# Sixteen-head cross attention: one exponential per score bank, the next scores behind the first of a unit's two, and another order of an item's jobs

## The chip, the cores and the metric

The kernel runs on one core of a Trainium2 chip. The metric is the device time of one execution in microseconds (us). TensorE (PE) multiplies matrices, with its weight loads listed apart as PEld; VectorE is DVE, ScalarE is ACT, GpSimd is POOL, and SyncE (SP) issues transfers. The engines run their own queues in order and meet at semaphores.

## What is computed

The whole program is two layers of a perceiver: x holds 32 items of 64 tokens by 128 features, and the context `ctx_1024` holds 32 items of 1601 tokens by 128. The change touches one of its six parts, the cross attention of the second layer with 16 heads of 8 features:

```python
H, dk = (N_HEADS, D_K)            # 16, 8
Q = (x_q @ W_Q + b_Q).reshape(B, L, H, dk).transpose(0, 2, 1, 3)
K = (x_k @ W_K + b_K).reshape(B, S, H, dk).transpose(0, 2, 1, 3)
V = (x_v @ W_V + b_V).reshape(B, S, H, dk).transpose(0, 2, 1, 3)
scores = jnp.einsum('bhld,bhsd->bhls', Q, K) / jnp.sqrt(jnp.float32(dk))
attn = jax.nn.softmax(scores, axis=-1)
ctx = jnp.einsum('bhls,bhsd->bhld', attn, V)
out = ctx.transpose(0, 2, 1, 3).reshape(B, L, H * dk) @ W_O + b_O
```

Here `x_q` is the normalized x (L = 64) and `x_k`, `x_v` are the context (S = 1601), for B = 32 items. The other parts are an eight-head cross attention, two self attentions, a mixture of experts and a tree network.

## The kernel before

`cross_attention` serves the eight-head stage (`XA0`) and the sixteen-head stage (`XA1`). It goes through 32 items (`b`). The 1601 context tokens are 13 tiles of 128 (the last has 65). With 16 heads the scores of one tile against 64 tokens are 16 x 64 = 1024 columns, two banks of PSUM, and one tile is one **unit**: an item has `NE` = 13 units. The work of an item is cut into jobs, and the string `ORDERS[heads]` lists them:

- S x: `pe_scores` (L585 with 16 heads, L589 with 8), eight matmuls for unit x, four into each of its two banks; then ACT's `act_exp` (L636) reads both banks with one instruction of 1024 columns and writes the buffer `Pb`.
- P x: `pe_product` (L605), probabilities times values of unit x, summed over the item in one bank. P-1 is the last unit of the item before.
- M j: `pe_maxima` (L552), raw scores of 402 keys (or 395) for the next item, into two banks; DVE reduces them to maxima in `dve_maxima`, with one instruction where the two banks are neighbours (L709) and two where they are not (L706, L707). There are 16. After M15 `dve_shift` makes the shift of the exponent, and job R (`pe_shift_rows`, L568, copied by ACT L687 and DVE L732) puts it in as rows of the queries.
- V j: `pe_values` (L538), values of four tiles for the next item, evicted by ACT (L656). V0, V1 and V2 have four tiles each, V3 has one.
- K j: `pe_keys` (L523), keys for the item after the next, evicted by ACT (L646) and then by DVE (L695). The letter H marks DVE's part.

Every engine walks the same string and takes its own part of each job, so the string fixes the order on PE, ACT and DVE, and for POOL and SP the places at which they prepare and load. Nothing is reordered at run time: an instruction that waits holds up all behind it on its engine. ACT's part of S x is `act_exp`; at P-1 it copies out the item's sums (`act_output`, L668), once an item. SP issues the key transfers of an item (L772, L773) at H3 and a context load (L761) at V3.

The eight PSUM banks are split with 16 heads into 3 for scores, 1 for the sums and 4 for work (M, V, K, R), which go round in a ring; an M job takes two of them, so two M jobs can be in flight. An item takes 41 work banks, so its jobs sit one bank further in the next. The scores' ring has three banks: unit u uses banks 2u and 2u + 1 modulo 3. Two units need four banks, and `pe_scores` waits until the whole exponential of the unit before has ended:

```python
emptied_exp = unit(b, x) - (1 if att.score_banks == 3 else 2)
if emptied_exp >= 0:
    eng.wait_ge(exps, units + emptied_exp + 1)
```

`act_exp` also waits for the product of four units before, since `Pb` has four buffers. With 8 heads there are four score banks, and the wait reaches back two units.

Of the kernel before, what the change touches and what calls it, by code (L numbers as in the profile page):

```python
# [37 lines left out]
ROWS = 98  # L38
# [8 lines left out]


ORDERS = {
# [4 lines left out]

# [1 line left out]
class Attention:  # L56


    def __init__(self, name, heads, cross, masked=False, values_k=D):
# [25 lines left out]
        self.NE = len(self.exps)  # L85
        self.units = heads // 2
        self.halved = heads == 16
        q4 = 402
        self.kchunks = [(c * q4, min(q4, NK - c * q4)) for c in range(4)] if cross else []
        self.vjobs = [list(range(i, min(i + 4, len(self.tiles)))) for i in range(0, len(self.tiles), 4)]  # L90
# [103 lines left out]
def bass_perceiver_kernel(nc, xT, ctxT, wpack, bpack, experts, picks, trees, outT):  # L194
    ROUTED = nc.dram_tensor("routed", (E, N), F32, kind="Internal").ap()
    ctx = ExitStack()
    with ctx:
# [245 lines left out]
        def cross_attention(role, eng, att, part, bname, inputs_ready=None, banks_ready=None):  # L443
# [58 lines left out]
            def unit(b, x):  # L502
                return b * NE + x

            def score_banks(b, x):

                first, last = sorted((2 * unit(b, x) + i) % att.score_banks for i in range(2))
                return ps[:, first:last + 1:last - first, :]

            def buffer(b, x):  # L510
                return unit(b, x) % 4
# [60 lines left out]
            def pe_scores(b, x):  # L572
                if x == 0:
                    for by in att.freed[(b, "R", 0)]:
                        eng.wait_ge(*emptied((b, "R", 0), by))
                emptied_exp = unit(b, x) - (1 if att.score_banks == 3 else 2)
                if emptied_exp >= 0:
                    eng.wait_ge(exps, units + emptied_exp + 1)
                out = score_banks(b, x)
                for ti, tile in enumerate(att.exps[x]):  # L580
                    k0, n = att.tiles[tile]
                    for g in range(4):
                        if att.halved:
                            for h in range(2):
                                mm = nc.tensor.matmul(out[0:n, h, g * 128:(g + 1) * 128], KST[half[h], b % 3, g, k0:k0 + n],  # L585
                                                      QW[half[h], b % 3, g * 128:(g + 1) * 128], start=True, stop=True,
                                                      tile_position=(64 * h, 0))
                        else:
                            mm = nc.tensor.matmul(out[0:n, ti, g * 128:(g + 1) * 128], KST[0:ROWS, b % 3, g, k0:k0 + n],  # L589
                                                  QW[0:ROWS, b % 3, g * 128:(g + 1) * 128], start=True, stop=True)  # L590
                mm.then_inc(scores, 1)

            def pe_product(b, x):
                if x == 0:
# [2 lines left out]
                        eng.wait_ge(oev, items + b)  # L597
                    else:
                        eng.wait_ge(vones, 2 * past + 2)
                eng.wait_ge(exps, units + unit(b, x) + 1)  # L600
                for ti, tile in enumerate(att.exps[x]):
                    _, n = att.tiles[tile]
                    for r, quad, h0, nh, v0, oc in att.groups:
# [26 lines left out]
            def act_exp(b, x):  # L630
                n = att.tiles[att.exps[x][0]][1]
                banks = len(att.exps[x]) * att.W // 512
                if unit(b, x) >= 4:
                    eng.wait_ge(pv, units + unit(b, x) - 3)
                eng.wait_ge(scores, units + unit(b, x) + 1)
                nc.scalar.activation(Pb[0:n, buffer(b, x), 0:banks * 512].rearrange("p (a c) -> p a c", a=banks),  # L636
                                     score_banks(b, x)[0:n, 0:banks, :], ACT.Exp, scale=att.scale).then_inc(exps, 1)

            def act_keys(b, j):
                job = (b, "K", j)  # L640
# [1566 lines left out]
```

## Time and profile before

| | us |
|---|---|
| Median of 3 runs | 1993.44 |
| Lowest and highest | 1987.66, 1996.09 |
| Profiled execution, its own time | 1998.57 |
| Its span, first to last instruction | 1996.8 |
| Mean granted clock of TensorE, share of full | 0.944 |
| PE, DVE, ACT, POOL busy | 1784.8, 1389.0, 1228.5, 506.3 |

The profile is of one execution. A busy time is the time in which an engine had at least one instruction running. In timelines the first two numbers of a row are the start and the duration, "xN" is how many instructions were merged into it, and the bracket gives the engine's idle time before it with what released it. The stage of the change runs from about 1003 to 1719 us of the span.

### The profile page before, as it was taken

Reading aid. Unit: us, or ns where it says so; the run is one execution under the profiler, and the core shown is the slowest. Engines: PE = TensorE matmul, PEld = TensorE weight load, DVE = VectorE, ACT = ScalarE, POOL = GpSimd, SP = SyncE. Lnnn points to the kernel's source line nnn. Section 1 sums busy time; section 2 is a strip of 40 time slices with the busy share of each in tenths; the row PEclk is TensorE's granted clock in tenths of the full one; section 3 lists DMA queues with packets and bytes.
Section 4 is the critical chain, followed back from the end, with each engine's and each line's share of the span. In section 5 each row is a group of like instructions: output and inputs, shape, how many; then the busy total and the mean of one; then the engine's idle time right before and its main releaser. Section 6 shows DMA issues by size and latency. Waiting matters only on the chain. (4 is left out here: it accounts for less than half of the span.)

```text
span 1996.8 us, 67986 instructions
## 1 busy us (share of the span) xinstructions
PE 1784.8 (89%) x29656; PEld 1112.0 (56%) x29656; DVE 1389.0 (70%) x2411; ACT 1228.5 (62%) x1789; POOL 506.3 (25%) x399
## 2 busy tenths in 40 slices
PE   7899999999999576998599999999999998857898
PEld 5577777777755454443355555555555555525543
DVE  2577777777636654665688888888888887337565
ACT  3377777777733552332278777877787777338243
POOL 4322323222131511112112222222222220024265
PEclk8799999999999687999799999999999999778999
DMA  4355555555300301654645554555555551030011
GB/s 151 95 139 149 143 150 136 144 147 140 75 2 6 60 3 43 169 146 145 114 73 96 97 94 87 101 94 97 89 101 91 96 92 28 1 65 4 28 37 43
DMA packets 66549, 178.33 MB, mean 89 GB/s; under 512 B 20276, under 2 KB 24500, under 8 KB 65844
## 3 DMA queue, kind: packets, MB, share of 16 engines
q1 hardware_dynamic: 64436, 170.85, 38.9%
q8 instruction: 234, 3.83, 0.8%
q10 hardware_dynamic: 1824, 3.20, 0.8%
q14 instruction: 55, 0.45, 0.1%
HBM read 84.39 MB, written 1.31 MB: 43 GB/s over the span
## 5 line engine op out<-in xcount | busy, mean ns | idle before, releaser
L636 ACT ACTIVATE Pb<-ps 128x1024 f32<-128x1024 f32 (+2 forms) x640 | 630.5, 1001 | 187.2 <-PE ps L585 139.5
L709 DVE TENSOR_REDUCE MX<-ps 128x2 f32<-128x804 f32 (+1 forms) x386 | 369.0, 985 | 51.3 <-PE ps L552 46.6
L605 PE MATMUL ps<-Pb,V 128*17 128x64 f32 (+1 forms) x13312 | 365.2, 249 | 0.2 <-ACT Pb L636 0.2
L605 PEld LDWEIGHTS ps<-Pb,V 128*17 128x17 f32 (+1 forms) x13312 | 251.8, 98 | 83.5 <-issue 69.4
L711 DVE TENSOR_REDUCE MX<-ps 128x1 f32<-128x402 f32 (+1 forms) x512 | 265.6, 568 | 30.2 <-PE ps L556 24.2
L753 POOL TENSOR_TENSOR ABO<-CT 128x1601 bf16<-128x1601 f32 x44 | 125.9, 2863 | 565.6 <-DMA CT<-ctxT 565.6
L552 PE MATMUL ps<-KST,QW 50*128 50x402 bf16 (+1 forms) x1024 | 176.1, 342 | 22.4 <-ACT V L656 11.1
L585 PE MATMUL ps<-QW,KST 50*128 50x128 bf16 (+1 forms) x3328 | 167.1, 220 | 30.9 <-ACT Pb L636 23.9
L585 PEld LDWEIGHTS ps<-QW,KST 50*128 50x128 bf16 (+1 forms) x3328 | 96.4, 96 | 125.6 <-ACT Pb L636 93.1
L656 ACT ACTIVATE V<-ps 128x512 f32<-128x512 f32 (+1 forms) x256 | 130.9, 514 | 40.2 <-PE ps L538 30.2
L556 PE MATMUL ps<-KST,QW 96*128 96x402 bf16 (+1 forms) x512 | 148.4, 339 | 5.5 <-DVE C L695 0.7
L538 PE MATMUL ps<-WS,ABO 128*128 128x128 bf16 (+1 forms) x832 | 132.3, 220 | 0.0
L589 PE MATMUL ps<-QW,KST 98*128 98x128 bf16 (+1 forms) x1664 | 124.5, 219 | 2.1 <-ACT Pb L636 1.6
L695 DVE SCALAR_TENSOR_TENSOR HL<-ps,W,HL 128x402 bf16<-128x402 f32 (+1 forms) x128 | 77.1, 632 | 60.6 <-ACT HL L646 58.8
L538 PE MATMUL ps<-WS,CT 128*128 128x128 bf16 (+1 forms) x1144 | 117.5, 222 | 0.1
L589 PEld LDWEIGHTS ps<-QW,KST 98*128 98x128 bf16 (+1 forms) x1664 | 108.5, 99 | 16.3 <-ACT Pb L636 2.3
L695 DVE SCALAR_TENSOR_TENSOR C<-ps,W,C 128x402 bf16<-128x402 f32 (+1 forms) x128 | 77.1, 632 | 51.4 <-ACT C L646 49.1
L552 PEld LDWEIGHTS ps<-KST,QW 50*128 50x128 bf16 x1024 | 51.2, 93 | 97.0 <-issue 40.5
L538 PEld LDWEIGHTS ps<-WS,CT 128*128 128x128 bf16 (+1 forms) x1144 | 89.2, 100 | 22.9 <-issue 8.9
L1549 ACT ACTIVATE Pb<-ps 128x512 f32<-128x512 f32 x68 | 40.5, 597 | 98.3 <-PE ps L1509 92.8
L1509 PE MATMUL ps<-ABO 128*128 128x512 bf16 x384 | 95.4, 385 | 3.7 <-DVE Pb L1558 3.7
L523 PE MATMUL ps<-CT,WS 128*128 128x402 bf16 (+1 forms) x336 | 90.4, 351 | 6.0 <-ACT V L656 5.5
(246 smaller groups left out, 2986.3 us busy)
## 6 DMA issues: line engine op xcount, KB each, us to landing
CT<-ctxT SPq DMA_DIRECT2D x44, 800.5 KB, 4.8
KST<-HL SPq DMA_DIRECT2D x320, 100.1 KB, 2.9
KST<-C SPq DMA_DIRECT2D x320, 100.1 KB, 3.0
Pb<-routed SPq DMA_DIRECT2D x64, 256.0 KB, 4.0
ABO<-ctxT SPq DMA_DIRECT2D x10, 800.5 KB, 5.3
T<-ctxT SPq DMA_DIRECT2D x10, 800.5 KB, 4.5
KST<-HL SPq DMA_DIRECT2D x128, 50.0 KB, 2.7
KST<-C SPq DMA_DIRECT2D x128, 50.0 KB, 2.7
```

Of the source, the lines that this page charges most:

```text
L538: mm = nc.tensor.matmul(work(job)[0:n, i * D:(i + 1) * D], still[:, k0:k0 + n], WS[:, 1, wp, :], start=(k == 0), stop=(k == 2))
L552: mm = nc.tensor.matmul(work(job)[:, h, 0:n], QW[half[h], b % 3, g * 128:(g + 1) * 128], KST[half[h], b % 3, g, c0:c0 + n], start=True, st ...
L556: mm = nc.tensor.matmul(work(job)[:, 0:n], QW[0:RAW, b % 3, g * 128:(g + 1) * 128], KST[0:RAW, b % 3, g, c0:c0 + n], start=True, stop=True)
L585: mm = nc.tensor.matmul(out[0:n, h, g * 128:(g + 1) * 128], KST[half[h], b % 3, g, k0:k0 + n], QW[half[h], b % 3, g * 128:(g + 1) * 128], ...
L589: mm = nc.tensor.matmul(out[0:n, ti, g * 128:(g + 1) * 128], KST[0:ROWS, b % 3, g, k0:k0 + n], QW[0:ROWS, b % 3, g * 128:(g + 1) * 128], s ...
L605: mm = nc.tensor.matmul(ps[32 * quad:32 * quad + m, SUM, oc:oc + nh * S], V[0:n, b % 2, tile, v0:v0 + m], Pb[0:n, buffer(b, x), ti * att.W ...
L636: nc.scalar.activation(Pb[0:n, buffer(b, x), 0:banks * 512].rearrange("p (a c) -> p a c", a=banks), score_banks(b, x)[0:n, 0:banks, :], AC ...
L656: nc.scalar.activation(V[0:n, b % 2, ts[0]:ts[0] + len(ts), 0:att.NV].rearrange("p t (h e) -> p t h e", h=att.H)[:, :, :, 0:att.d], work(j ...
L695: nc.vector.scalar_tensor_tensor(keys(b)[:, 1, c0:c0 + n], work(job)[:, 0:n], bias(f"bk{t[-1]}"), keys(b)[:, 0, c0:c0 + n], ALU.add, ALU.s ...
L709: nc.vector.reduce_max(MX[:, b % 2, 2 * j:2 * j + 2], work(job)[:, :, 0:n], AX.X).then_inc(freed["dve"], 1)
L711: nc.vector.reduce_max(MX[:, b % 2, j:j + 1], work(job)[:, 0:n], AX.X).then_inc(freed["dve"], 1)
L753: nc.gpsimd.tensor_tensor(context_lo(b), context(b), context_hi(b), ALU.subtract).then_inc(sem("cross_low"), 1)
```

## The change

Three edits, all for 16 heads.

1. `act_exp` issues one exponential of 512 columns for each of the two banks, each raising `exps` by one. `parts` is the number of exponentials in a unit, and `scored` turns a unit and a number of its parts into a semaphore value. `pe_product` waits for both parts.
2. `pe_scores` waits for the first exponential of the unit before (and, by the queue's order, for all of earlier units), in place of its only one. The first bank of the new unit is the third of the ring, and its second bank is the one that this first exponential has read.
3. `ORDERS[16]` is another string with the same jobs.

```diff
-    16: ("M0 K0 H0 K1 H1 S0 M1 P-1 K2 H2 K3 H3 S1 V0 M2 S2 V1 M3 S3 M4 P0 M5 S4 M6 P1 M7 S5 P2 P3 M8 S6 M9 P4 P5 S7 "
-         "M10 M11 P6 S8 M12 P7 M13 S9 V2 M14 S10 M15 P8 P9 S11 P10 V3 R0 S12 P11 "),
+    16: ("M0 K0 H0 K1 S0 H1 M1 P-1 K2 K3 S1 H2 H3 V0 M2 V1 S2 M3 P0 M4 S3 P1 M5 S4 M6 P2 S5 M7 P3 M8 S6 "
+         "P4 M9 S7 M10 P5 S8 M11 P6 M12 S9 P7 M13 S10 M14 P8 M15 S11 P9 P10 S12 V2 V3 R0 P11 "),
...
+        self.parts = 2 if self.halved else 1
...
+            def score_bank(b, x, i):
+
+                return ps[:, (2 * unit(b, x) + i) % att.score_banks, :]
...
+            def scored(b, x, parts):
+
+                return exps, units + att.parts * unit(b, x) + parts
...
-                emptied_exp = unit(b, x) - (1 if att.score_banks == 3 else 2)
-                if emptied_exp >= 0:
-                    eng.wait_ge(exps, units + emptied_exp + 1)
-                out = score_banks(b, x)
+                if unit(b, x):
+                    if att.halved:
+                        eng.wait_ge(*scored(b, x - 1, 1))
+                    elif unit(b, x) > 1:
+                        eng.wait_ge(*scored(b, x - 2, 1))
...
-                                mm = nc.tensor.matmul(out[0:n, h, g * 128:(g + 1) * 128], KST[half[h], b % 3, g, k0:k0 + n],
+                                mm = nc.tensor.matmul(score_bank(b, x, h)[0:n, g * 128:(g + 1) * 128], KST[half[h], b % 3, g, k0:k0 + n],
...
-                eng.wait_ge(exps, units + unit(b, x) + 1)
+                eng.wait_ge(*scored(b, x, att.parts))
...
-                nc.scalar.activation(Pb[0:n, buffer(b, x), 0:banks * 512].rearrange("p (a c) -> p a c", a=banks),
-                                     score_banks(b, x)[0:n, 0:banks, :], ACT.Exp, scale=att.scale).then_inc(exps, 1)
+                if att.halved:
+                    for i in range(2):
+                        nc.scalar.activation(Pb[0:n, buffer(b, x), i * 512:(i + 1) * 512], score_bank(b, x, i)[0:n, :],
+                                             ACT.Exp, scale=att.scale).then_inc(exps, 1)
+                else:
+                    nc.scalar.activation(Pb[0:n, buffer(b, x), 0:banks * 512].rearrange("p (a c) -> p a c", a=banks),
+                                         score_banks(b, x)[0:n, 0:banks, :], ACT.Exp, scale=att.scale).then_inc(exps, 1)
```

Lines of the changed kernel are numbered 9 to 15 higher around the stage: scores are L595 (L585 before), products L615 (L605), maxima L561 (L552), values L547 (L538), keys L532 (L523), the exponential L648 (L636), ACT's values L671 (L656), keys L661 (L646), shift rows L702 (L687) and output L683 (L668).

**ACT over one item, before.** From the shift rows of one item to those of the next (Pb is the exponential, V values, HL or C keys, OE the output).

```order
L687 ACTIVATE QW<-ps 2x512
L636 ACTIVATE Pb<-ps 65x1024
L646 ACTIVATE HL<-ps,W 128x402 x2
L636 ACTIVATE Pb<-ps 128x1024
L668 ACTIVATE OE<-ps 128x256
L646 ACTIVATE HL<-ps,W 128x402
L646 ACTIVATE HL<-ps,W 128x395
L636 ACTIVATE Pb<-ps 128x1024
L656 ACTIVATE V<-ps 128x64x8
L636 ACTIVATE Pb<-ps 128x1024
L656 ACTIVATE V<-ps 128x64x8
L636 ACTIVATE Pb<-ps 128x1024 x7
```

and now:

```order
L702 ACTIVATE QW<-ps 2x512
L661 ACTIVATE HL<-ps,W 128x402 x2
L648 ACTIVATE Pb<-ps 128x512 x2
L683 ACTIVATE OE<-ps 128x256
L661 ACTIVATE HL<-ps,W 128x402
L661 ACTIVATE HL<-ps,W 128x395
L648 ACTIVATE Pb<-ps 128x512 x2
L671 ACTIVATE V<-ps 128x64x8 x2
L648 ACTIVATE Pb<-ps 128x512 x20
L648 ACTIVATE Pb<-ps 65x512 x2
```

The exponential is two instructions of 512 columns. V0 and V1 now stand together ahead of unit 2's exponentials, eleven units follow without another job between (units 2 to 12, twenty-two instructions), and V2 and V3 come together behind unit 12's; before, V1 stood behind unit 2, V2 behind unit 9, and V3 and the shift rows ahead of unit 12.

**PE in the middle of an item, before.** From the scores of unit 5 to the product ahead of those of unit 8 (L585 scores, L605 products, L552 maxima).

```order
L585 MATMUL ps<-QW,KST 128x128 x8
L605 MATMUL ps<-Pb,V 18x128 x16
L552 MATMUL ps<-KST,QW 128x402 x2
L585 MATMUL ps<-QW,KST 128x128 x8
L552 MATMUL ps<-KST,QW 128x402 x2
L605 MATMUL ps<-Pb,V 18x128 x16
L585 MATMUL ps<-QW,KST 128x128 x8
L552 MATMUL ps<-KST,QW 128x402 x2
L552 MATMUL ps<-KST,QW 128x395 x2
L605 MATMUL ps<-Pb,V 18x128 x8
```

and now, the same stretch of an item (L595, L615, L561):

```order
L595 MATMUL ps<-QW,KST 128x128 x8
L561 MATMUL ps<-KST,QW 128x395 x2
L615 MATMUL ps<-Pb,V 18x128 x8
L561 MATMUL ps<-KST,QW 128x402 x2
L595 MATMUL ps<-QW,KST 128x128 x8
L615 MATMUL ps<-Pb,V 18x128 x8
L561 MATMUL ps<-KST,QW 128x402 x2
L595 MATMUL ps<-QW,KST 128x128 x8
L561 MATMUL ps<-KST,QW 128x402 x2
L615 MATMUL ps<-Pb,V 18x128 x8
L595 MATMUL ps<-QW,KST 128x128 x8
```

Between two scores jobs there are now one or two maxima jobs and one product in every turn, where before some turns held two products and no maxima, others two maxima.

**PE at the end of an item, before.** From the scores of unit 11 to those of unit 12 and the product behind.

```order
L585 MATMUL ps<-QW,KST 128x128 x8
L605 MATMUL ps<-Pb,V 18x128 x8
L538 MATMUL ps<-WS,T 65x128 x2
L538 MATMUL ps<-WS,CL 65x128
L568 MATMUL ps<-WB,MH 2x128 x8
L585 MATMUL ps<-QW,KST 65x128 x8
L605 MATMUL ps<-Pb,V 18x128 x8
```

and now (L547 values, L577 shift rows):

```order
L595 MATMUL ps<-QW,KST 128x128 x8
L615 MATMUL ps<-Pb,V 18x128 x16
L595 MATMUL ps<-QW,KST 65x128 x8
L547 MATMUL ps<-WS,T 128x128 x2
L547 MATMUL ps<-WS,CL 128x128
```

Unit 12's scores now stand behind two products and ahead of V2, V3 and the shift rows.

## Rows read from the trace of the kernel before

**Rows 1.** The page, part 1: busy time, share of span, instructions.

```profile
PE 1784.8 (89%) x29656; PEld 1112.0 (56%) x29656; DVE 1389.0 (70%) x2411; ACT 1228.5 (62%) x1789; POOL 506.3 (25%) x399
```

**Rows 2.** One line's instructions, outputs of items (L668), 1040 to 1690.

```profile
L668 ACT ACTIVATE OE<-ps x29: 377/395/395, 1050.1 to 1674.7; 128x256 f32<-128x256 f32 x29
```

**Rows 3.** Busy time by stretch: steady items, last item; header names columns.

```profile
core 0: us, PE busy (x) PEld busy (x) DVE busy (x) ACT busy (x) POOL busy (x), PEclk, DMA share, GB/s
1049.90:1673.00 623.10, 589.44 (x11252) 351.11 (x11250) 526.58 (x782) 492.80 (x642) 138.20 (x139) 1.00 0.53 92
1697.00:1718.60 21.60, 16.01 (x296) 9.59 (x296) 0.00 (x0) 12.19 (x14) 0.52 (x2) 0.66 0.01 2
```

**Rows 4.** Waits, 1050 to 1650: us in total, times, longest us.

```profile
ACT Pb L636 <- PE ps L585: 112.7, 190, 0.8
PEld ps L585 <- ACT Pb L636: 71.2, 230, 0.7
DVE MX L709 <- PE ps L552: 38.6, 86, 0.8
```

**Rows 5.** Timeline, one middle turn: start us, duration us, engine, line.

```profile
1303.07 0.40 PE L585 MATMUL ps<-QW,KST 50*128 50x128 bf16 x8
...
1303.39 1.07 PE L605 MATMUL ps<-Pb,V 128*18 128x128 f32 x32
1303.57 1.02 ACT L636 ACTIVATE Pb<-ps 128x1024 f32<-128x1024 f32 x1 [0.56 <-PE ps L585]
...
1304.40 0.34 PE L552 MATMUL ps<-KST,QW 50*128 50x402 bf16 x2
...
1304.65 0.40 PE L585 MATMUL ps<-QW,KST 50*128 50x128 bf16 x8
1304.78 0.99 DVE L709 TENSOR_REDUCE MX<-ps 128x2 f32<-128x804 f32 x1 [0.24 <-PE ps L552]
```

**Rows 6.** Timeline of ACT, end of one item, start of the next.

```profile
1310.80 0.59 ACT L656 ACTIVATE V<-ps 128x512 f32<-128x512 f32 x1
1311.46 1.02 ACT L636 ACTIVATE Pb<-ps 128x1024 f32<-128x1024 f32 x1
1313.31 1.02 ACT L636 ACTIVATE Pb<-ps 128x1024 f32<-128x1024 f32 x1 [0.83 <-PE ps L585]
...
1316.39 1.08 ACT L646 ACTIVATE HL<-ps,W 128x402 bf16<-128x402 f32 x2 [0.24 <-PE ps L523]
...
1321.12 1.03 ACT L636 ACTIVATE Pb<-ps 128x1024 f32<-128x1024 f32 x1
```

**Rows 7.** Timeline of ACT, eight-head and expert stages.

```profile
303.42 1.94 ACT L636 ACTIVATE Pb<-ps 128x1024 f32<-128x1024 f32 x2 [0.27 <-PE ps L589]
...
879.45 0.60 ACT L1549 ACTIVATE Pb<-ps 128x512 f32<-128x512 f32 x1 [1.56 <-PE ps L1509]
879.94 0.41 ACT L1538 ACTIVATE ABO<-CT 128x256 bf16<-128x256 f32 x1
```

**Rows 8.** DVE: timeline in one item, then its groups, 1050 to 1650.

```profile
1299.80 4.74 DVE L709 TENSOR_REDUCE MX<-ps 128x2 f32<-128x790 f32 x5 [0.60 <-PE ps L552]
...
1311.92 0.57 DVE L706 TENSOR_REDUCE MX<-ps 128x1 f32<-128x395 f32 x1
...
1312.99 0.19 DVE L717 TENSOR_REDUCE MG<-MX 128x8 f32<-128x32 f32 x1
...
1314.42 0.70 DVE L732 CAST QW<-ps 2x512 bf16<-2x512 f32 x1 [0.83 <-PE ps L568]
...
1317.02 1.18 DVE L695 SCALAR_TENSOR_TENSOR HL<-ps,W,HL 128x402 bf16<-128x402 f32 x2 [0.28 <-ACT HL L646]
...
L709 DVE TENSOR_REDUCE MX<-ps 128x2 f32<-128x804 f32 (+1 forms) x322 | 308.6, 985 | 42.9 <-PE ps L552 38.6
...
L706 DVE TENSOR_REDUCE MX<-ps 128x1 f32<-128x402 f32 (+1 forms) x109 | 62.0, 569 | 13.8 <-PE ps L552 11.4
```

**Rows 9.** Timeline of ACT, last item.

```profile
1701.86 1.02 ACT L636 ACTIVATE Pb<-ps 128x1024 f32<-128x1024 f32 x1 [0.76 <-PE ps L585]
```

More of the change, by code:

```diff
@@ L588, in pe_scores @@
                         else:
-                            mm = nc.tensor.matmul(out[0:n, ti, g * 128:(g + 1) * 128], KST[0:ROWS, b % 3, g, k0:k0 + n],
+                            mm = nc.tensor.matmul(score_bank(b, x, ti)[0:n, g * 128:(g + 1) * 128], KST[0:ROWS, b % 3, g, k0:k0 + n],
                                                   QW[0:ROWS, b % 3, g * 128:(g + 1) * 128], start=True, stop=True)
```

## The prediction

> **What bounds the kernel now.** The page comes first: TensorE is busy 89% of the span, VectorE 70%, ScalarE 62% [rows 1]. Those shares mix many stages, and the change is confined to one, the sixteen-head cross attention, so I read that stage alone. 28 intervals between outputs of items last 624.6 us, so an item takes 22.31 us [rows 2]. In 623.1 us of this stage (27.9 items) PE is busy 589.4, DVE 526.6 and ACT 492.8 us: 21.1, 18.9 and 17.6 us an item at the full granted clock [rows 3]. No engine is full. PE's 21.1 flatters it, because the drain of the last matmul before a wait counts as busy.
>
> The waits say what holds the item together [rows 4]: ACT's exponential waits for scores 112.7 us (190 times), and the scores' weight loads wait for the exponential 71.2 us (230 times). Each waits for the other. That is a loop, and the timeline shows one turn of it [rows 5]: scores start at 1303.07, the exponential 0.50 later at 1303.57, lasts 1.02, ends at 1304.59, and the next scores start 0.06 later at 1304.65. One turn is 1.58 us. Thirteen turns are 20.5 us of the item's 22.31; in the rest ACT is dense with evictions. From the exponential of unit 11 (1313.31) to that of the next item's unit 2 (1321.12) pass 7.81 us in which ACT idles only 0.24 [rows 6]. I call this the tail; the other 22.31 - 7.81 = 14.50 us, unit 2 to unit 11, are the middle, where the loop sets the pace.
>
> **What the change does, part by part.**
>
> *The exponential in halves.* 416 instructions of 1024 columns become 832 of 512. Two full ones back to back last 1.94 us, one 1.02, so a full one occupies ACT for 0.92. A 512-column activation of the expert stage lasts 0.60 and its follower starts 0.49 after it [rows 7]. Two halves then occupy 0.98, which is 0.06 more per unit, 0.8 us an item on ACT. The bounds are 0 more, and 0.66 for each half, the spacing at which a value eviction holds up the exponential behind it [rows 6], which would make 1.32 for a pair. I take 0.49, since the row has the same width and a plain contiguous output. The Trainium skill (ScalarE: Activation LUTs, What ACT_TABLE_LOAD costs) gives 186 ns plus 0.833 ns a column with 93 ns of overlap; an estimate from it is 0.52 a half, 1.04 a pair, about 1.2 us an item instead of 0.8. No wait of the loop depends on which is right.
>
> *The earlier start.* Scores of the next unit need the first half and the free third bank alone. The turn becomes 0.60 + 0.06 + 0.50 = 1.16 us instead of 1.58, and ACT's 0.98 fits in it. Nine turns of the middle would take 10.4 us instead of 14.2. The second half ends 0.49 + 0.60 = 1.09 after the first starts, against 1.02 now; products that wait for it run two units behind, so these 0.07 us cost nothing, and their cover is more than a turn.
>
> *What is late next: VectorE.* Thirteen maxima jobs (M3 to M15) now stand between scores 2 and scores 11. Five in a row last 4.74 us, 0.948 each; a job whose two banks are not neighbours goes as two instructions, 1.07 us from 1311.92 to 1312.99, 0.12 more, and 109 of 431 jobs are such, one in four [rows 8]. Two jobs are in flight, so scores 11, behind M15, need M13 reduced: eleven reductions are 11 x 0.948 + 2.75 x 0.12 = 10.8 us. Before and behind them: M3's reduction can begin about 0.1 before the exponential of unit 2 (its fill goes out right behind the scores and takes 0.38 to its reduction [rows 5]; it is held a little by value bank V0); 0.1 of stall at M5; then 0.05 release, 0.26 for M15's fill and 0.50 to the exponential. The middle becomes 11.6 us. It is DVE's pace, not the loop's 10.4.
>
> *The order.* V1 moves ahead of S2 and V2 behind S12. Both evictions leave the middle, where ACT had room, for the tail, where it has none. Tail occupancy is 7.81 - 0.24 = 7.57; add 2 x 0.66 for them and 4 x 0.06 for the halved exponentials: 9.1. Add idle: S12 now stands behind two products, which puts it 0.32 + 1.01 behind S11 [rows 5], so exponential 12 comes 1.33 after exponential 11 while ACT is free after 0.98: 0.35. For K0 waiting on the bank that V3 frees I add another 0.3, an estimate from the 0.24 now before the same job. The tail becomes 9.8 us, 2.0 longer than now. PE's R0 waits for DVE's shift as now (the copy behind it finds DVE 0.83 us idle [rows 8]); the key evictions on DVE (1.18 a pair) keep their place beside this.
>
> *Queues.* SP issues the same 16 transfers an item behind H3 and one context load behind V3, POOL the same five operations. H3 and V3 stay in the tail, and what they load is read an item later, so I cost them at nothing; their cover is most of an item, and if it went, M0 would wait for its keys.
>
> *The last item* has no maxima and runs at a mean granted clock of 0.66 [rows 3]; a turn there takes up to 1.02 + 0.76 = 1.78 us [rows 9]. I take 0.3 to 0.4 off each of 12 turns, -4 us.
>
> **The sum.** 9.8 + 11.6 = 21.4 us an item; I take 21.5, leaving 0.1 for odd and even bank positions. That is 0.8 less, for 31 items -25 us, with the last item -29. The eight-head stage is not touched: its waits come out the same. The profiled execution took 1998.57 us (span 1996.8) and becomes 1969.6; it lay 5.1 above the median of the three runs, 1993.44, so against that median the forecast is about 1965. An item of 21.2 to 21.9 us gives -34 to -13, with the last item's -4 in all -38 to -17, or 1955 to 1977.
>
> **The rivals.**
>
> *VectorE's refills stop mattering.* DVE needs 18.9 us an item. If its other idle falls to about 1.5 us, an item is 20.4: 31 x -1.9 - 4 = -63, or 1930. For it: the loop no longer delays PE's fills. Against: ACT's tail of 9.1 and eleven reductions are already 19.9 without one gap.
>
> *The halves do not overlap.* At 0.60 a half, 1.20 a pair, the tail's occupancy is 9.1 + 4 x 0.22 = 10.0, its idle 0.1 and 0.3, together 10.4; the middle's 9 x 1.20 = 10.8 still hide under DVE's 11.6. The item takes 22.0: -10 - 4, or 1980. At 0.66 the tail is 10.8, the middle 9 x 1.32 = 11.9, the item 22.7: +12 - 4, or 2001. I put the case at 1990. Against: the 0.49 of rows 7. The Trainium skill (Perfetto Trace Analysis, Optimizing Scalar/DVE Operations) says that grouping into larger operations helps if the engine is saturated, and that breaking up helps if it is not but causes bubbles on others. The rows show both here: bubbles in the middle, a saturated ACT in the tail.
>
> *The middle does not pay for the tail* (slower). The tail grows by 2.0 for certain, as two evictions move into it. The middle must fall from 14.5 below 12.5 to break even. It does not if PE, in one queue, reaches each fill late: the spare between a free bank pair and DVE running dry is one reduction less the release and fill, 0.95 - 0.05 - 0.38 = 0.5 us, while a product and a scores job in between take about 0.8. If DVE's present wait for maxima fills, 38.6 us in 27 items or 1.4 each [rows 4], comes on top, the middle is 13.0 and the item 22.8: 31 x 0.5 - 4 = +12, or 2005. Against: that wait is for fills standing behind blocked scores, which is what the change unblocks.
>
> *The early start is not used.* Should PE arrive at each scores job later than the whole exponential ends, the edit frees nothing and only the order counts. Against: nearly every middle turn is the bare 1.58. I count it with the last two.
>
> **How the numbers follow.** A measurement of this kernel tells about 0.5%, 10 us, from no change. Forecast 0.62; faster rival 0.12; no overlap 0.12; slower rival 0.14. The forecast and the fast rival are faster, with a few hundredths of the middle cases: 0.77. Within 0.5%: 0.12. Slower: 0.11, as part of the last rival lands inside 10 us. The range reaches halfway to each outer case: 1940 to 1991.
>
> **What would show it.** The interval between outputs should be 21.5 (right between 21.2 and 21.9). The halves should last 0.60 at 0.49 apart, and the middle's turns should be irregular, 1.2 to 1.5, with DVE nearly gapless. ACT's wait for scores should fall from 4 us an item to about 1.5, the scores' wait for exponentials to under 1. The tail should be near 9.8. A middle over 12.5 makes the forecast wrong by the slow rival, halves 0.6 apart by the third case, and an item under 21 by the first.

## The result, and the profile after

The changed kernel takes 1933.7 us (median of 4 runs, 1932.7 to 1942.7) against 1993.3 before; the ratio is 0.971, with a 95% interval of 0.968 to 0.975. It is faster by 59.6 us, where 28 were forecast: the sign was right, the time lies below the range of 1940 to 1991, and the gain is twice the forecast. It is close to the 1930 of the rival in which VectorE's refills stop mattering.

The page of the profiled execution (1934.0 us, span 1932.2), part 1, beside [rows 1]:

```profile
PE 1755.1 (91%) x29638; PEld 1107.3 (57%) x29656; DVE 1378.2 (71%) x2412; ACT 1253.0 (65%) x2205; POOL 506.0 (26%) x399
```

The outputs of items, beside [rows 2]: 32 outputs, so 31 intervals from the first to the last.

```profile
L683 ACT ACTIVATE OE<-ps x32: 384/405/405, 1017.6 to 1652.1; 128x256 f32<-128x256 f32 x32
```

(1652.1 - 1017.6) / 31 is 20.47 us an item, where before it was 22.27. The last interval is 15.0 us, before 22.3; the 30 ahead of it are 20.65 in the mean. The last items have less and less work for items to come, so a steady item is best taken from the outputs between 1050 and 1600 us: 20.74 now, 22.33 before. As in [rows 3], steady items and the last one:

```profile
1050.00:1600.00 550.00, 539.19 (x10677) 334.13 (x10671) 492.70 (x743) 488.40 (x956) 132.98 (x134) 1.00 0.57 100
1637.10:1652.10 15.00, 11.63 (x300) 7.18 (x296) 0.00 (x0) 13.33 (x27) 1.22 (x3) 1.00 0.01 3
```

In the steady stretch PE is busy 98% of the time (before 95%), DVE 90% (before 85%) and ACT 89% (before 79%). Who waited for whom, 1050 to 1600, beside [rows 4]:

```profile
PEld ps L595 <- ACT Pb L648: 32.8, 159, 0.5
ACT Pb L648 <- PE ps L595: 24.7, 85, 0.8
...
DVE MX L724 <- PE ps L561: 14.4, 40, 0.6
```

Per item (26.6 of them in the 550 us) ACT waits for scores 0.9 us, before 4.2; the scores wait for the exponential 1.2, before 2.6; DVE waits for maxima fills 0.5, before 1.4. ACT's timeline over one item, beside [rows 5, 6]:

```profile
1301.81 1.08 ACT L648 ACTIVATE Pb<-ps 128x512 f32<-128x512 f32 x2 [0.55 <-PE ps L595]
1303.15 1.08 ACT L648 ACTIVATE Pb<-ps 65x512 f32<-65x512 f32 x2 [0.26 <-PE ps L595]
...
1305.96 1.08 ACT L661 ACTIVATE C<-ps,W 128x402 bf16<-128x402 f32 x2 [0.47 <-PE ps L532]
...
1311.50 10.51 ACT L648 ACTIVATE Pb<-ps 128x512 f32<-128x512 f32 x18
1322.37 1.08 ACT L648 ACTIVATE Pb<-ps 128x512 f32<-128x512 f32 x2 [0.36 <-PE ps L595]
```

Eighteen halves, units 2 to 10, go in 10.51 us without an idle time that the view names, so eight turns from unit 2 to unit 10 in 10.51 - 1.08 = 9.43, the loop's pace of 1.18 each. The tail, exponential 11 (1301.81) to exponential 2 (1311.50), is 9.69 us; the middle, to the next exponential 11 (1322.37), is 10.87. DVE over the same middle:

```profile
1311.55 11.88 DVE L724 TENSOR_REDUCE MX<-ps 128x2 f32<-128x790 f32 x13 [0.53 <-PE ps L561]
```

Thirteen reductions in one piece, 11.88 us, 0.908 us from one to the next. In the next item the bank pairs are neighbours only every other time:

```profile
1332.10 0.98 DVE L724 TENSOR_REDUCE MX<-ps 128x2 f32<-128x790 f32 x1 [0.53 <-PE ps L561]
1333.00 0.57 DVE L721 TENSOR_REDUCE MX<-ps 128x1 f32<-128x402 f32 x1
1333.48 0.57 DVE L722 TENSOR_REDUCE MX<-ps 128x1 f32<-128x402 f32 x1
...
1342.37 0.56 DVE L721 TENSOR_REDUCE MX<-ps 128x1 f32<-128x402 f32 x1
```

From M3 (1332.10) to M14 (1342.37) eleven reductions take 10.27 us with five split ones among them, where 11 x 0.908 is 9.99: a split one costs 0.06 more. That item's middle, 1332.05 to 1343.17, is 11.12 us, the next two are 10.93 and 11.19 by the same view.

Where the 64.6 us between the two profiled executions are: the stage's 31 intervals went from 690.4 to 634.5 us, 55.9; from the first exponential to the first output 1.4. The other 7.3 are not the change's: the stage began 8.8 us earlier (first exponential at 996.2, before 1005.0) and what follows it took 1.5 longer, in code that is the same. Over all profiled executions of this study the first exponential lies between 989.9 and 1008.1 us, with no relation to the edit. So from here on I compare kernels by the mean interval between outputs as well as by their times.

### The profile page after: what moved, and what is told of

Its sections match the earlier page's. It is cut to its first block and busy times, and to the rows that moved or that the text cites. A ratio compares the mean times of both kernels' runs of the same rounds, so it can differ in the third digit from the quotient of the medians.

```text
span 1932.2 us, 68384 instructions
## 1 busy us (share of the span) xinstructions
PE 1755.1 (91%) x29638; PEld 1107.3 (57%) x29656; DVE 1378.2 (71%) x2412; ACT 1253.0 (65%) x2205; POOL 506.0 (26%) x399
## 5 line engine op out<-in xcount | busy, mean ns | idle before, releaser
L648 ACT ACTIVATE Pb<-ps 128x512 f32<-128x512 f32 (+1 forms) x832 | 451.9, 597 | 49.7 <-PE ps L595 30.7
L615 PE MATMUL ps<-Pb,V 128*17 128x64 f32 (+1 forms) x13312 | 379.5, 248 | 0.7 <-ACT Pb L648 0.7
L724 DVE TENSOR_REDUCE MX<-ps 128x2 f32<-128x804 f32 (+1 forms) x385 | 363.7, 983 | 18.5 <-PE ps L561 17.3
L615 PEld LDWEIGHTS ps<-Pb,V 128*17 128x17 f32 (+1 forms) x13312 | 250.1, 97 | 86.8 <-issue 43.3
L651 ACT ACTIVATE Pb<-ps 128x1024 f32<-128x1024 f32 (+1 forms) x224 | 204.6, 959 | 40.9 <-PE ps L599 38.2
L561 PE MATMUL ps<-KST,QW 50*128 50x402 bf16 (+1 forms) x1024 | 177.4, 342 | 13.3 <-DVE MX L724 5.6
L595 PE MATMUL ps<-QW,KST 50*128 50x128 bf16 (+1 forms) x3328 | 164.9, 218 | 5.4 <-ACT Pb L648 3.6
L671 ACT ACTIVATE V<-ps 128x512 f32<-128x512 f32 (+1 forms) x256 | 129.3, 522 | 49.4 <-PE ps L547 39.8
L595 PEld LDWEIGHTS ps<-QW,KST 50*128 50x128 bf16 (+1 forms) x3328 | 104.2, 95 | 74.0 <-ACT Pb L648 45.4
L547 PE MATMUL ps<-WS,ABO 128*128 128x128 bf16 (+1 forms) x832 | 131.2, 220 | 0.0
L547 PE MATMUL ps<-WS,CT 128*128 128x128 bf16 (+1 forms) x1144 | 114.3, 221 | 3.3 <-DVE HL L710 1.6
L547 PEld LDWEIGHTS ps<-WS,CT 128*128 128x128 bf16 (+1 forms) x1144 | 90.0, 100 | 23.2 <-issue 12.4
L561 PEld LDWEIGHTS ps<-KST,QW 50*128 50x128 bf16 x1024 | 51.5, 93 | 88.4 <-issue 40.0
```

The source lines that it names most:

```text
L547: mm = nc.tensor.matmul(work(job)[0:n, i * D:(i + 1) * D], still[:, k0:k0 + n], WS[:, 1, wp, :], start=(k == 0), stop=(k == 2))
L561: mm = nc.tensor.matmul(work(job)[:, h, 0:n], QW[half[h], b % 3, g * 128:(g + 1) * 128], KST[half[h], b % 3, g, c0:c0 + n], start=True, st ...
L595: mm = nc.tensor.matmul(score_bank(b, x, h)[0:n, g * 128:(g + 1) * 128], KST[half[h], b % 3, g, k0:k0 + n], QW[half[h], b % 3, g * 128:(g ...
L615: mm = nc.tensor.matmul(ps[32 * quad:32 * quad + m, SUM, oc:oc + nh * S], V[0:n, b % 2, tile, v0:v0 + m], Pb[0:n, buffer(b, x), ti * att.W ...
L648: nc.scalar.activation(Pb[0:n, buffer(b, x), i * 512:(i + 1) * 512], score_bank(b, x, i)[0:n, :], ACT.Exp, scale=att.scale).then_inc(exps, 1)
L671: nc.scalar.activation(V[0:n, b % 2, ts[0]:ts[0] + len(ts), 0:att.NV].rearrange("p t (h e) -> p t h e", h=att.H)[:, :, :, 0:att.d], work(j ...
```

## The experiments

All times are medians, with the ratio to runs of the kernel before on the same chip; beside experiments 1 to 4 that kernel took 1992.0 us, beside 5 to 8 1989.9 and beside 9 to 11 1985.7, so kernels of different groups are better compared by the ratio. "Item" is the last output minus the first, over 31. "Steady" is the mean interval between the outputs from 1050 to 1600 us. It leaves out the last item, in which the granted clock differs from one profiled execution to another. Both are of one profiled execution each.

| Kernel | us | ratio (95%) | item, us | steady, us |
|---|---|---|---|---|
| before | 1993.3 | 1 | 22.27 | 22.33 |
| changed | 1933.7 | 0.971 (0.968 to 0.975) | 20.47 | 20.74 |
| 1 halves, old order | 1965.5 | 0.987 (0.985 to 0.989) | 21.57 | 21.81 |
| 2 whole exponential, new order | 2040.7 | 1.024 (1.022 to 1.027) | 23.85 | 24.04 |
| 3 halves, scores wait for the second | 2067.6 | 1.038 (1.035 to 1.040) | 24.65 | 24.76 |
| 4 short maxima | 1914.7 | 0.960 (0.958 to 0.963) | 20.05 | 20.30 |
| 5 V2 back in the middle | 1946.8 | 0.979 (0.976 to 0.982) | 20.95 | 21.18 |
| 6 V1 back in the middle | 1944.3 | 0.977 (0.974 to 0.979) | 20.78 | 21.02 |
| 7 product 10 behind V3 | 1938.3 | 0.975 (0.972 to 0.978) | 20.55 | 20.85 |
| 8 the same, K0 ahead of M0 | 2011.7 | 1.012 (1.009 to 1.016) | 22.46 | 22.97 |
| 9 short products | 1927.0 | 0.970 (0.966 to 0.973) | 20.25 | 20.47 |
| 10 short products and maxima | 1901.6 | 0.957 (0.952 to 0.962) | 19.72 | 19.86 |
| 11 products 10 and 11 later | 1938.1 | 0.974 (0.969 to 0.978) | 20.70 | 20.97 |

**1. The early start without the order.** The changed kernel with the old string for 16 heads.

> The changed kernel with the old order of jobs. Theory A (the early start makes the gain, and moving V1 and V2 out of the middle was not needed): the tail falls back to about 7.9 us, the middle's loop is 9 turns of 1.16 us plus about 0.5 for each of V1 and V2, 11.4 to 11.8, so an item takes 19.3 to 19.8 us and the kernel about 1905 to 1920 us, faster than the changed kernel at 1933.7. Rival B (the even spacing of the new order is what lets VectorE run without a gap): turns with two products or two maxima jobs make fills late, the middle stays at 12.5 to 13, the item at 20.6 to 21.5, the kernel at 1935 to 1960 us.

Rival B's side, and past its end: 1965.5 us, 21.57 an item. ACT in one middle:

```profile
1302.17 1.14 ACT L648 ACTIVATE Pb<-ps 128x512 f32<-128x512 f32 x2
...
1307.01 1.08 ACT L648 ACTIVATE Pb<-ps 128x512 f32<-128x512 f32 x2 [0.47 <-PE ps L595]
1308.51 1.08 ACT L648 ACTIVATE Pb<-ps 128x512 f32<-128x512 f32 x2 [0.41 <-PE ps L595]
...
1316.42 1.08 ACT L648 ACTIVATE Pb<-ps 128x512 f32<-128x512 f32 x2 [0.68 <-PE ps L595]
...
1324.02 1.14 ACT L648 ACTIVATE Pb<-ps 128x512 f32<-128x512 f32 x2
```

The tail is 7.60 us (1316.42 to 1324.02), as short as I said, but the middle is 14.25 (1302.17 to 1316.42), hardly less than the 14.5 before. A turn there is 1.50 (1307.01 to 1308.51), not 1.16. PE behind the same turn:

```profile
1306.52 0.39 PE L595 MATMUL ps<-QW,KST 50*128 50x128 bf16 x8
1306.84 1.07 PE L615 MATMUL ps<-Pb,V 128*18 128x128 f32 x32
1307.84 0.34 PE L561 MATMUL ps<-KST,QW 50*128 50x402 bf16 x2
1308.02 0.39 PE L595 MATMUL ps<-QW,KST 50*128 50x128 bf16 x8
```

The scores, two products and a maxima job follow each other without idle time: 0.32 + 1.00 + 0.18 = 1.50. The loop is open, but where the old order has two products in a turn, PE's own work is longer than the loop. Other turns wait for VectorE or for an eviction. Three waits, 1050 to 1600:

```profile
DVE MX L724 <- PE ps L561: 30.2, 72, 0.5
...
PEld ps L561 <- DVE MX L724: 25.1, 95, 0.5
PE ps L561 <- ACT V L671: 17.5, 44, 0.7
```

DVE waits for fills 30.2 us where the changed kernel has 14.4. PE's maxima wait 25.1 us for reductions, there 13.8, and 17.5 us for a value eviction on ACT. So the early start alone earns 0.7 us an item of the 1.8 (0.5 of 1.6 in steady items).

**2. The order without the early start.** The kernel before with the new string.

> The kernel before with the new order of jobs: one exponential of 1024 columns, scores wait for all of it. Theory A (the loop of scores and exponential sets the middle): the middle is 9 turns of 1.58 = 14.2 us, the tail 9.7 less four times 0.06, the item 23.6 to 23.8 us, the kernel about 1993 + 31 x 1.4 = 2030 to 2040 us. Rival B (the order itself carries part of the gain by keeping VectorE fed): the item stays at 22.3 or less, 1980 to 1995 us.

Theory A, just past the upper end of its range: 2040.7 us, 23.85 an item. The turns are the old 1.58:

```profile
1302.23 1.02 ACT L636 ACTIVATE Pb<-ps 128x1024 f32<-128x1024 f32 x1 [0.56 <-PE ps L585]
1303.81 1.02 ACT L636 ACTIVATE Pb<-ps 128x1024 f32<-128x1024 f32 x1 [0.56 <-PE ps L585]
```

Alone, the order loses 1.6 us an item: it lengthens the tail and the loop keeps the middle.

**3. Two halves, late release.**

```diff
-                        eng.wait_ge(*scored(b, x - 1, 1))
+                        eng.wait_ge(*scored(b, x - 1, 2))
```

> The changed kernel, but scores wait for the second half of the unit before. Theory A (only the early release gains): a turn is 0.49 + 0.60 + 0.06 + 0.50 = 1.65 us, the middle 14.9, the tail 9.7, the item 24.5 us, the kernel 2055 to 2070 us. Rival B (it is the order, or the smaller instruction, that gains): under 1980 us.

Theory A again: 2067.6 us, 24.65 an item, turns of 1.64:

```profile
1304.43 1.09 ACT L648 ACTIVATE Pb<-ps 128x512 f32<-128x512 f32 x2 [0.55 <-PE ps L595]
1306.07 1.08 ACT L648 ACTIVATE Pb<-ps 128x512 f32<-128x512 f32 x2 [0.55 <-PE ps L595]
```

Experiments 2 and 3 differ by the second instruction alone: 0.80 us an item, 0.73 in steady items, and the prediction's price was 13 x 0.06 = 0.8. Experiment 3 and the changed kernel differ by the semaphore value alone: 24.65 - 20.47 = 4.2 us an item, 4.0 in steady items. The early start is worth that in the new order and, by experiment 1 against before, no more than 1.5 in the old one (the 0.7 and the 0.8 that the halves cost).

**4. VectorE relieved.** A reduction over half of each job's columns.

```diff
+                if att.halved:
+                    n = n // 2
                 if last - first > 1:
```

> The changed kernel, but the maxima of the sixteen-head stage are taken over the first half of each job's columns (201 of 402), so a reduction on VectorE takes about 0.4 us less; the shift of the exponent is then a maximum over half of the keys. Theory A (VectorE's pace sets the middle at 11.0 us): the middle falls to the loop's 10.4, the tail by 0.2 to 0.5, the item from 20.7 to 19.6 to 19.9 us, the kernel from 1933.7 to 1900 to 1912 us. Rival B (the loop of scores and first half sets it, VectorE only fills its time): under 0.2 us an item, 1926 to 1934 us.

1914.7 us, 20.05 an item: 0.4 less, between the theories' figures, 3 us outside A's. ACT and VectorE in one item:

```profile
1301.53 11.68 ACT L648 ACTIVATE Pb<-ps 128x512 f32<-128x512 f32 x20
...
1321.80 2.23 ACT L648 ACTIVATE Pb<-ps 128x512 f32<-128x512 f32 x4
```

```profile
1302.38 0.58 DVE L726 TENSOR_REDUCE MX<-ps 128x2 f32<-128x402 f32 x1 [0.27 <-PE ps L561]
1303.45 1.06 DVE L726 TENSOR_REDUCE MX<-ps 128x2 f32<-128x402 f32 x2 [0.50 <-PE ps L561]
```

With DVE idle before most reductions, as here, the halves of units 2 to 11 go in one piece: 20 of them in 11.68 us, 1.18 a turn. The middle is 10.6, which is the loop, and the tail remains 9.7. So VectorE held the middle of the changed kernel only by its last 0.3 to 0.6 us, and does not hold the tail.

**5 and 6. One value job back in the middle.**

```diff
-         "P4 M9 S7 M10 P5 S8 M11 P6 M12 S9 P7 M13 S10 M14 P8 M15 S11 P9 P10 S12 V2 V3 R0 P11 "),
+         "P4 M9 S7 M10 P5 S8 M11 P6 M12 S9 V2 P7 M13 S10 M14 P8 M15 S11 P9 P10 S12 V3 R0 P11 "),
```

> The changed kernel with value job V2 back behind scores 9, as in the kernel before; V3 stays behind scores 12. Theory A (a value job in the middle holds a work bank behind ACT's halves and puts 0.7 us of filling in front of PE's maxima jobs, so VectorE runs dry): the tail loses 0.66, the middle gains 0.9 to 1.3, the item is 0.3 to 0.6 us longer, the kernel 1943 to 1953 us. Rival B (an eviction costs the same wherever it stands, and in the middle ACT has 0.2 us of slack in every turn): the item is 0 to 0.4 us shorter, 1921 to 1934 us.

```diff
-    16: ("M0 K0 H0 K1 S0 H1 M1 P-1 K2 K3 S1 H2 H3 V0 M2 V1 S2 M3 P0 M4 S3 P1 M5 S4 M6 P2 S5 M7 P3 M8 S6 "
+    16: ("M0 K0 H0 K1 S0 H1 M1 P-1 K2 K3 S1 H2 H3 V0 M2 S2 V1 M3 P0 M4 S3 P1 M5 S4 M6 P2 S5 M7 P3 M8 S6 "
```

> The changed kernel with value job V1 back behind scores 2. Theory A (its fill then stands between scores 2 and M3, VectorE's first reduction of the middle starts up to 0.9 us later against exponential 2, and the eviction lengthens one turn): tail -0.7, middle +0.9 to +1.1, the item 0.2 to 0.4 us longer, 1940 to 1947 us. Rival B (as much is saved in the tail as is lost in the middle): 1930 to 1937 us.

Theory A for both by the time: 1946.8 and 1944.3 us; V2's item is 0.5 us longer than the changed kernel's, V1's 0.3. V2 in the middle, on DVE and on ACT:

```profile
1322.13 1.00 DVE L724 TENSOR_REDUCE MX<-ps 128x2 f32<-128x804 f32 x1 [0.88 <-PE ps L561]
```

```profile
1322.42 1.09 ACT L648 ACTIVATE Pb<-ps 128x512 f32<-128x512 f32 x2 [0.53 <-PE ps L595]
```

VectorE runs dry for 0.88 us behind V2, and ACT stands idle 0.53 us before exponential 10. V1 costs a gap of 0.81 us before exponential 3:

```profile
1320.40 0.67 ACT L671 ACTIVATE V<-ps 128x512 f32<-128x512 f32 x1
1321.89 3.38 ACT L648 ACTIVATE Pb<-ps 128x512 f32<-128x512 f32 x6 [0.81 <-PE ps L595]
```

From exponential 11 to exponential 2 the same views give a tail of 9.14 us in experiment 5 and 8.74 in 6, against 9.69. So the two moves lengthen the tail by 0.55 and 0.95 us, and earn 0.5 and 0.3 more than that in the middle. If the two simply add, they are 0.8 of the 1.1 us by which the new order improves on experiment 1. The rest may be the even spacing of products and maxima, for which the turn of 1.50 above speaks; it was not tried by itself.

**7, 8 and 11. Attempts at a faster order.** Each changes only places of jobs in the string of the changed kernel.

Experiment 7, and the second line of 8:

```diff
-         "P4 M9 S7 M10 P5 S8 M11 P6 M12 S9 P7 M13 S10 M14 P8 M15 S11 P9 P10 S12 V2 V3 R0 P11 "),
+         "P4 M9 S7 M10 P5 S8 M11 P6 M12 S9 P7 M13 S10 M14 P8 M15 S11 P9 S12 V2 V3 P10 R0 P11 "),
```

The first line of 8:

```diff
-    16: ("M0 K0 H0 K1 S0 H1 M1 P-1 K2 K3 S1 H2 H3 V0 M2 V1 S2 M3 P0 M4 S3 P1 M5 S4 M6 P2 S5 M7 P3 M8 S6 "
+    16: ("K0 H0 M0 K1 S0 H1 M1 P-1 K2 K3 S1 H2 H3 V0 M2 V1 S2 M3 P0 M4 S3 P1 M5 S4 M6 P2 S5 M7 P3 M8 S6 "
```

Experiment 11:

```diff
-    16: ("M0 K0 H0 K1 S0 H1 M1 P-1 K2 K3 S1 H2 H3 V0 M2 V1 S2 M3 P0 M4 S3 P1 M5 S4 M6 P2 S5 M7 P3 M8 S6 "
-         "P4 M9 S7 M10 P5 S8 M11 P6 M12 S9 P7 M13 S10 M14 P8 M15 S11 P9 P10 S12 V2 V3 R0 P11 "),
+    16: ("M0 K0 H0 K1 S0 H1 M1 P-2 P-1 K2 K3 S1 H2 H3 V0 M2 V1 S2 M3 P0 M4 S3 P1 M5 S4 M6 P2 S5 M7 P3 M8 S6 "
+         "P4 M9 S7 M10 P5 S8 M11 P6 M12 S9 P7 M13 S10 M14 P8 M15 S11 P9 S12 V2 V3 R0 P10 "),
```

> A try at a faster one: the changed kernel with product 10 behind V3 in place of ahead of scores 12, so that scores 12 start 0.5 us earlier. In the trace of the changed kernel ACT is idle 0.26 us before the exponential of unit 12, and the eviction of V2 follows it directly. Theory A (the tail is ACT's chain): the tail loses 0.2 to 0.3 us, the kernel 6 to 9 us, 1925 to 1928 us. Rival B (VectorE's shift rows R, or the keys behind them, set the tail): no change, 1932 to 1935 us.

> The same and K0 with its part on VectorE ahead of M0. K0 then takes a bank that is free already, where now ACT idles 0.47 us before its eviction. Theory A: ACT's tail loses up to 0.4 us more, 1913 to 1922 us. Rival B: VectorE waits for K0's eviction before it can take M0's maxima, M1 and the rest come 0.5 us later, and it eats the gain or more: 1925 to 1940 us.

> A try at a faster one: the changed kernel with product 10 behind the shift rows and product 11 behind M1 of the next item, ahead of product 12, so that scores 12, values, shift rows and keys come up to 1.0 us earlier on TensorE. Theory A (the place of the products in the tail holds ACT up before exponential 12, 0.26 us, and before K0's eviction, 0.47 us): the item loses 0.3 to 0.6 us, the kernel 1915 to 1925 us. Rival B (TensorE is full in the tail, and what moves ahead pushes the products into K2 and scores 1): 1930 to 1938 us, as the product behind V3 alone gave.

None beats the changed kernel; 7 ends past both of its theories, 11 at Rival B's upper end. In 7 exponential 12 follows 11 without idle time, and the keys come no earlier:

```profile
1305.37 2.24 ACT L648 ACTIVATE Pb<-ps 128x512 f32<-128x512 f32 x4 [0.55 <-PE ps L595]
...
1309.63 1.08 ACT L661 ACTIVATE C<-ps,W 128x402 bf16<-128x402 f32 x2 [0.76 <-PE ps L532]
```

The keys' eviction starts 4.26 us after exponential 11; in the changed kernel it is 4.15 (1301.81 to 1305.96). ACT wins 0.26 us and waits 0.76 in place of 0.47. What PE has to do between scores 11 and K0 is the same in another order; that this decides is argued, and experiments 9 and 11 fit it. Theory A was right about ACT's idle time and wrong that it is worth anything. Experiment 11 takes a product out of that stretch; the keys' eviction then comes 3.96 us after exponential 11, but what left the stretch is paid behind it, and an item is 20.70. Experiment 8 is slower than the kernel before, outside both of its ranges: 22.46 us an item, 1.9 more than 7, for K0 and its part on VectorE ahead of M0. ACT waits for what had stood ready:

```profile
1314.78 0.38 ACT L683 ACTIVATE OE<-ps 128x256 f32<-128x256 f32 x1 [0.89 <-PE ps L615]
1315.72 0.59 ACT L661 ACTIVATE HL<-ps,W 128x402 bf16<-128x402 f32 x1 [0.56 <-PE ps L532]
```

By the string, DVE takes M0 only behind K0's eviction and M1 comes later by that; behind M1's fill on PE stand the product, for which the output waits 0.89 us, and the keys, 0.56. But not all of the 1.9 us is this chain. PE in the same item, and the four microseconds from M1's fill on:

```profile
1313.80 0.35 PE L561 MATMUL ps<-KST,QW 50*128 50x402 bf16 x2 [1.19 <-DVE MX L724]
```

```profile
1313.80:1318.20 4.40, 4.40 (x43) 2.53 (x44) 2.71 (x5) 2.54 (x6) 4.18 (x4) 0.62 0.00 0
```

Here the granted clock fell, to 0.62 in the mean; in the other kernels it is 1.00 from 1050 to 1600 us, in this one 0.97. The items with such a fall take 23.6 to 24.1 us, those without one (1044 to 1200 us) 22.3, and in the item before this one ACT waits only 0.22 for the keys. So the order itself costs 1.5 us an item more than experiment 7, three times my price of half a microsecond, and the lower clock the rest. Not every such wait of PE brings it: the item before has one of 1.26 us and keeps its clock. The other three executions were 12 to 23 us longer than the profiled one (1996.5), at a lower mean clock (0.929 to 0.931, here 0.942), so the 1.012 holds some of it too.

**9 and 10. TensorE relieved, alone and with VectorE.**

```diff
+                        cols = S if att.halved and tile else nh * S
-                            ps[32 * quad:32 * quad + m, SUM, oc:oc + nh * S], V[0:n, b % 2, tile, v0:v0 + m],
+                            ps[32 * quad:32 * quad + m, SUM, oc:oc + cols], V[0:n, b % 2, tile, v0:v0 + m],
```

> The changed kernel, but after the first tile each product multiplies 64 of its 128 columns, so half of the heads get sums of one tile alone; a product takes TensorE about 0.27 us in place of 0.5, some 2.8 us less an item. Theory A (TensorE, busy 98% of the steady stretch of the changed kernel, is by now the pace of the tail, where its own work adds up to about 9.0 of 9.7 us): the tail falls to 9.0 to 9.3, the middle by 0.1 or not at all, the item from 20.6 to 20.0 to 20.2, the kernel 1915 to 1922 us. Rival B (ACT's evictions and VectorE set the tail, TensorE only fills its time): 1929 to 1935 us.

> The short products and the short maxima (201 of 402 columns on VectorE) together. Theory A: only the loop of scores and first half is left in the middle, 9 turns of 1.17 = 10.6 us, and ACT's own time in the tail, 9.0: the item 19.5 to 19.7 us, the kernel 1895 to 1905 us. Rival B (the two gains are the same gain): no more than the short maxima alone, 1912 to 1916 us.

With a tenth of its work gone, TensorE's busy share in the steady stretch falls from 98% to 90%:

```profile
1050.00:1600.00 550.00, 495.33 (x10823) 299.49 (x10827) 497.18 (x753) 494.83 (x968) 133.12 (x134) 1.00 0.57 102
```

The time is 1927.0 us, between the two ranges and nearer to Rival B's; its ratio is 0.970 against 0.971 of the changed kernel, no difference that these runs can tell. The items do tell one: a steady item is 0.27 us shorter, 0.18 of it in the tail, where the keys' eviction comes 3.97 us after exponential 11. What hides it in the time is in part the last item, 16.4 us at a granted clock of 0.69 where the changed kernel has 15.0 at 1.00. So a tenth of TensorE's work, about 1.9 us an item, is worth 0.27: most of its 98% is not on the path. Both relieved give 19.72 an item and 0.957, Theory A by the time, against 20.05 and 0.960 with the maxima alone. The intervals of the two ratios overlap, and only the items tell them apart, by 0.44 us in steady ones. The last item is slower here too:

```profile
1610.30:1627.80 17.50, 14.33 (x300) 8.85 (x296) 0.00 (x0) 13.35 (x27) 1.22 (x3) 0.52 0.01 2
```

What is left in the steady items is the loop in the middle and the chain through ACT and PE in the tail.

## Why the prediction was right in its cause and wrong in its size

*The loop* was right. Experiments 2 and 3 hold it at 1.58 and 1.64 and lose 49 and 76 us against the kernel before; with the early release 18 halves go at 1.18 a turn, forecast 1.16. The halves last 0.60, two last 1.08 to 1.09, 0.49 apart, as taken from [rows 7]; their price of 0.8 us an item is what experiments 2 and 3 show. The estimate that the prediction made from the Trainium skill (ScalarE: Activation LUTs, What ACT_TABLE_LOAD costs) was 1.2 us an item; the measured price is two thirds of it. The Trainium skill's advice to break up instructions where ACT is not saturated but causes bubbles on others (Perfetto Trace Analysis, Optimizing Scalar/DVE Operations) fits what happened: ACT was 79% busy before and is 89% now, and the item is shorter.

*The tail* came out right, 9.8 forecast and 9.69 measured, but partly by luck. Its idle times are 0.26 before exponential 12 (forecast 0.35), 0.47 before K0 (forecast 0.3) and 0.28 before V1's eviction, for which the sum had nothing. That is 1.01 where I had 0.65. ACT's own work is 9.69 - 1.01 = 8.68 where I had 9.1, for the most part because a value eviction does not always hold up its follower by 0.66: V1's, at 1311.00, lets exponential 2 start at 1311.50.

*The middle is the step that failed*: "eleven reductions are 11 x 0.948 + 2.75 x 0.12 = 10.8 us". They take 9.99 us in one item and 10.27 in the next, 10.1 in the mean. So the bound was named rightly, since shorter reductions do shorten the middle (experiment 4), but its pace was priced 0.7 us too high. The middle lies only 0.3 to 0.6 us above the loop's 10.6, not 1.2 above its 10.4, and the turns are not irregular, as I had said, but at the loop's pace up to exponential 10 in the item shown. The 0.948 came from dividing a merged row of five [rows 8] by its count. Such a row still holds idle times too short for the view to name; probably PE's fills were late in it. The row of four in the same item of the kernel before would have told:

```profile
1306.83 3.69 DVE L709 TENSOR_REDUCE MX<-ps 128x2 f32<-128x804 f32 x4 [0.15 <-PE ps L552]
```

Without the last one's duration, (3.69 - 0.98) / 3 is 0.90. The split pair's 1.07 was measured where its successor waited for it; in a row it costs 0.06 more and not 0.12. Both sizes were taken too high, and both stood on the engine that I had just named the new bound. Two small terms were off as well: the 0.1 of stall at M5 did not come, and M3's reduction began 0.05 behind exponential 2, not 0.1 ahead of it. With 0.05 + 10.1 + 0.81 for release, fill and scores, the sum gives 11.0, and four items measure 11.03 in the mean.

I then rounded the sum up by 0.1 to 21.5, where 20.7 was measured in steady items. Of these 0.8 us the middle is 0.6, and the tail and the rounding are 0.1 each. On 30 or 31 items that is about 25 us of the 31 by which the time lies below 1965.

*The last item* is the other step that failed: "0.3 to 0.4 off each of 12 turns, -4 us". It lost 7.4: 22.3 us before, 15.0 now. The loop by itself takes 1.58 - 1.16 = 0.42 off a turn, 5 us in 12. Of the rest, 2.1 us were turns longer than 1.58 in the kernel before (eleven in 19.5 us), nearly all at the lower clock, and I had kept part of that. PE in the last item of the kernel before, and of the changed one:

```profile
1697.58 0.61 PE L585 MATMUL ps<-QW,KST 50*128 50x128 bf16 x8 [1.18 <-ACT Pb L636]
1699.37 0.61 PE L585 MATMUL ps<-QW,KST 50*128 50x128 bf16 x8 [1.18 <-ACT Pb L636]
...
1707.15 0.40 PE L585 MATMUL ps<-QW,KST 50*128 50x128 bf16 x8
```

```profile
1641.47 0.40 PE L595 MATMUL ps<-QW,KST 50*128 50x128 bf16 x8 [0.19 <-ACT Pb L648]
...
1642.63 0.40 PE L595 MATMUL ps<-QW,KST 50*128 50x128 bf16 x8 [0.19 <-ACT Pb L648]
```

Before, the scores took 0.61 us at the lower level for part of the item, mean granted clock 0.66 [rows 3]; now they take 0.40 throughout, the granted clock of the stretch is 1.00, and a turn is 1.15. With the same waits experiments 9 and 10 had 0.69 and 0.52 there, so this share of the gain is not one that the edit brings each time.

*The rivals.* The fast one (12%) gave nearly the right time, with an item of 20.4 for a measured 20.7 and a last item that gained 4 for 7.4. Its premise was that DVE's idle time would fall to about 1.5 us an item; it fell from 3.4 to 2.1 (10% of 20.65), so it was mostly right, and my objection to it rested on the same reductions that I had priced too high. The slower one did not come: PE does not reach fills late in the new order (0.5 us of wait an item, before 1.4), but it does in the old one, in experiment 1. There, too, some turns are as the last rival had it: PE comes to the scores when its two products are done, whatever the exponential released. The halves do overlap. *The range* was too narrow by 6 us, because the reductions, the largest term of the sum, had no bounds of their own in it.

What stays open: how much of the order's gain is the even spacing by itself, what sets the granted clock in the last item, and why the untouched part ahead of the stage varies by 18 us between executions.

## What to carry to other kernels

Where two engines wait for each other in turn, splitting one engine's instruction at a buffer boundary and releasing the partner after the first part can be worth several times its price, here 4.2 us an item for 0.8. It only shows if the order of the other jobs keeps the next engine in line fed: the early start alone gained 0.7 us, the order alone lost 1.6, together they gained 1.8, so such edits have to be tried together. When the next bound is named, take its pace from starts in an unbroken run, not from a merged row divided by its count. And look at the granted clock before an item's length is read as the price of an edit: experiments 8, 9 and 10 each held a part that was clock.

## What the hardware showed that I had not expected

The last item has no maxima, keys or values in either kernel. Before, TensorE was busy 16.0 of 21.6 us in it, with idle times of up to 1.2 us between its jobs, and the granted clock was 0.66; now it is busy 11.6 of 15.0, idle 0.19 us in most turns, and the clock is 1.00. It would be easy to say that the shorter turns brought the clock back, but the other executions do not bear it out. Over its last item the granted clock was 1.00 in experiments 7 and 11, 0.89 in 4, 5, 6 and 8, 0.80 in 1, 0.76 in 2, 0.69 in 9, 0.56 in 3 and 0.52 in 10. Experiments 9 and 10 have the early start and the new order as the changed kernel has them, and only less work. So the last item gave 3.4 us more than I had forecast in this execution, and why is not shown.

The other surprise is how little a busy share says. With a tenth of TensorE's work gone its share fell from 98% to 90%, and a steady item from 20.74 to 20.47 us.
